# A recurrent layer in fp32: the input parts and the output matmuls on column tiles of 64 in place of 32

## The reference

```python
Xz, Xr, Xh = X @ Wxz.T + bxz, X @ Wxr.T + bxr, X @ Wxh.T + bxh   # for all steps
def step(H, (xz, xr, xh)):
    Z = sigmoid(xz + H @ Whz.T + bhz)
    R = sigmoid(xr + H @ Whr.T + bhr)
    H_tilda = tanh(xh + (R * H) @ Whh.T + bhh)
    H_new = Z * H + (1 - Z) * H_tilda
    Y = H_new @ Whq.T + bhq
out = x + Y                                                       # x is [32, 256, 256]
```

## Time and profile before

| | |
|---|---|
| Median of 3 runs | 524.92 us (524.47 to 526.99) |
| Profiled execution: time, span | 523.88 us, 522.0 us |
| TensorE matmul busy | 510.2 us, 98%, 44184 records |
| Weight load busy | 492.3 us, 94%, 44184 records |
| VectorE, ScalarE busy | 317.6 us (61%), 329.2 us (63%) |
| DMA over the span | 53 GB/s |

### The profile page before, as it was taken

One profiled execution on the slowest core, in us unless ns is written; L12 is line 12 of the kernel. 1 busy time (PEld: TensorE's weight loads), 2 busy tenths in 40 slices (PEclk: granted clock), 3 DMA queues, 4 the chain that ended last, 5 costly groups with the idle time before them and its releaser, 6 DMA issues.

```text
span 522.0 us, 96066 instructions
## 1 busy us (share of the span) xinstructions
PE 510.2 (98%) x44184; PEld 492.3 (94%) x44184; DVE 317.6 (61%) x1929; ACT 329.2 (63%) x1800; POOL 0.2 (0%) x4
## 2 busy tenths in 40 slices
PE   8499999999999999999999999999999999999997
PEld 7499999999999999999999999999999999999997
DVE  1266666666666666666666666666666666666665
ACT  2266666666666666666666666666666666666665
POOL 0000000000000000000000000000000000000000
PEclk9999999999999999999999999999999999999999
DMA  5111121111111111111221111111111111111111
GB/s 176 29 51 45 50 55 46 50 55 45 51 55 45 51 54 45 52 54 45 53 53 45 55 51 45 54 51 45 55 50 45 55 51 45 55 50 45 55 50 51
DMA packets 57735, 27.63 MB, mean 53 GB/s; under 512 B 6784, under 2 KB 56832, under 8 KB 57728
## 3 DMA queue, kind: packets, MB, share of 16 engines
q1 hardware_dynamic: 56880, 26.70, 18.4%
q10 hardware_dynamic: 848, 0.83, 0.5%
HBM read 18.98 MB, written 8.52 MB: 53 GB/s over the span
## 4 chain that ended last, share of the span: by engine, by line
PE 96%; issue 2%; DMA 1%; SPq 0%; DVE 0%; ACT 0%; ACTq 0%; DVEq 0%
PE r_ps L244 34%; PE c_ps L244 28%; PE z_ps L244 23%; PE y_ps L244 11%; DMA whq_sb<-in_whq_dram 1%; SPq L114 0%; SPq L115 0%; SPq L116 0%; SPq L112 0%; DVE u_sb L230 0%; DVE o_sb L212 0%; DVE h_sb L235 0%; ACT c_sb L189 0%; DVE rh_sb L225 0%; ACT r_sb L179 0%
## 5 line engine op out<-in xcount | busy, mean ns | idle before, releaser
L244 PE MATMUL c_ps<-xt_sb,wx_sb 128*32 128x64 f32 (+1 forms) x4104 | 172.8, 225 | 1.5 <-issue 1.5
L244 PE MATMUL z_ps<-xt_sb,wx_sb 128*32 128x64 f32 (+1 forms) x4104 | 163.3, 220 | 0.0
L179 ACT ACTIVATE r_sb<-r_ps 128x32 f32<-128x32 f32 x512 | 91.3, 198 | 106.1 <-PE r_ps L244 98.7
L225 DVE TENSOR_TENSOR rh_sb<-r_sb,h_sb 128x32 f32<-128x32 f32 x512 | 89.8, 192 | 85.3 <-ACT r_sb L179 81.1
L244 PE MATMUL z_ps<-h_sb,whz_sb 128*32 128x32 f32 x8192 | 123.9, 198 | 2.2 <-issue 2.2
L244 PE MATMUL c_ps<-rh_sb,whh_sb 128*32 128x32 f32 x8192 | 122.6, 198 | 2.2 <-issue 1.9
L244 PE MATMUL y_ps<-whq_sb,h_sb 128*32 128x128 f32 x2064 | 113.5, 279 | 0.3 <-DVE h_sb L235 0.3
L244 PEld LDWEIGHTS z_ps<-h_sb,whz_sb 128*32 128x32 f32 x8192 | 108.7, 110 | 2.4 <-issue 2.4
L244 PE MATMUL r_ps<-xt_sb,wx_sb 128*32 128x64 f32 (+1 forms) x4104 | 108.2, 219 | 0.0
L230 DVE SCALAR_TENSOR_TENSOR u_sb<-z_sb,c_sb 128x32 f32<-128x32 f32 x512 | 75.2, 188 | 53.5 <-ACT c_sb L189 53.5
L244 PEld LDWEIGHTS z_ps<-xt_sb,wx_sb 128*32 128x32 f32 (+1 forms) x4104 | 101.1, 110 | 0.0
(11 more groups left out here) (27 smaller groups left out, 359.3 us busy)
## 6 DMA issues: line engine op xcount, KB each, us to landing
xt_sb<-in_xt_dram SPq DMA_DIRECT2D x130, 64.0 KB, 1.8
xres_sb<-in_xr_dram SPq DMA_DIRECT2D x130, 64.0 KB, 1.8
out_dram<-o_sb SPq DMA_DIRECT2D x130, 64.0 KB, 1.6
wx_sb<-in_wx_dram SPq DMA_DIRECT2D x3, 256.0 KB, 3.4
whr_sb<-in_whr_dram ACTq DMA_DIRECT2D x1, 256.0 KB, 5.0
whz_sb<-in_whz_dram ACTq DMA_DIRECT2D x1, 256.0 KB, 5.1
whh_sb<-in_whh_dram ACTq DMA_DIRECT2D x1, 256.0 KB, 5.6
whq_sb<-in_whq_dram SPq DMA_DIRECT2D x1, 256.0 KB, 6.4
```

The lines of the kernel that those rows point to most:

```text
L179: nc.scalar.activation(r_sb[:, o], r_ps[:, o, here], ACT.Sigmoid).then_inc(s_r[o], 1)
L225: nc.vector.tensor_tensor(rh_sb[:, k], r_sb[:, k], old[:, k], ALU.mult).then_inc(s_rh[k], 1)
L244: return nc.tensor.matmul(ps, weights, moving, start=start, stop=False, skip_group_check=True, **kw)
```

## The change

`columns` gets a width. The h-side groups keep 32; `x_piece` passes 64, so that an x group is two matmuls with weights of 128 x 64 in place of four of 128 x 32. `y_piece` issues two matmuls with both steps of the chunk as 64 weight columns. The moving operands, the sums, the places in PSUM, the waits and the order of the groups stay as they are. The x parts before the loop keep the full width.

```diff
-            def columns(ps, cols, w, k, o, moving, start=False):
-
-                for j in range(NQ):
-                    last = mm(ps[B * j:B * j + B, cols], w[:, k, P * o + B * j:P * o + B * j + B], moving,
-                              start=start, tile_position=(0, B * j))
+            def columns(ps, cols, w, k, o, moving, width=B):
+
+                for j in range(0, P, width):
+                    last = mm(ps[j:j + width, cols], w[:, k, P * o + j:P * o + j + width], moving, tile_position=(0, j))
                 return last
...
-                return columns(ps, cols, wx_sb[:, gate], k, o, xt_sb[:, p, k])
+                return columns(ps, cols, wx_sb[:, gate], k, o, xt_sb[:, p, k], width=W)
 
             def y_piece(p, k):
 
-                for j in range(NQ):
-                    half, step = divmod(j, CS)
-                    last = mm(y_ps[p][B * j:B * j + B, 0, 0:P], h_sb[:, k, CS * p + step], whq_sb[:, k, P * half:P * half + P],
-                              tile_position=(0, B * j))
+                for half in range(K):
+                    last = mm(y_ps[p][W * half:W * half + W, 0, 0:P], h_sb[:, k, CS * p:CS * p + CS],
+                              whq_sb[:, k, P * half:P * half + P], tile_position=(0, W * half))
                 return last
```

## The result

The change makes the kernel 48% slower: 779.24 us median (778.8 to 779.9, 4 runs) against 525.42 us (524.47 to 526.99, 4 runs), a ratio of 1.4827 with a 95% interval of 1.4802 to 1.4852. The prediction was 814 us, with 540 to 896 as range, and 0.82 for slower.

A forecast was written before the change was run, and what follows sets the result against it. TensorE's own work was taken to set the time in three steps of four, with the other engines close behind. Profiled 523.9 + 307.2 (switches) - 15.6 (u wait) - 1.2 (less code) = 814.3 us, range 540 to 896.

The forecast's parts named there:

- Instructions removed, at 0: Dropping 28 of 172 pairs a step in x and y groups saves nothing, since moving columns set their pace.
- Wider loads, at 0: Loads of 64 weight columns go side by side on two tiles, 0.111 us, hidden beneath the moving columns: cost 0.
- Rival 4: Loads of the two 64-wide tiles run one after another, x groups take 0.222 us: 674 us, chance 0.03.
- The switches, 2048 x 0.15 = 307 us: Eight changes between 32-wide and 64-wide tiles a step, around x and y runs, each cost TensorE 0.15 us.
- an inference: Switches between 32 and 64, and into wider tiles, cost the same as those seen from full width to 32.
- The sign that was named for the holes: In the timeline, idle time put down to issue, eight times a step, at starts about 0.2 us late.
- Rivals 1 and 2 (mixed freely): Tiles of 32 and 64 mix without loss: 524 us, chance 0.12; or seams also close: 515 us, chance 0.06.
- 3 (one direction): Only switches from wide to narrow pay: 661 us; chance 0.13, shared with smaller holes both ways.
- The 0.166 us: Fixed part of the single matmul latency, taken as one drain per switch: 340 us for all, about 847 us total.
- The cover of the u wait, -15.6 us: At step u == 0, switches between c groups and r take 0.6 us, so TensorE's 0.26 us wait for u disappears.
- Less code, -1.2 us: Four issue pauses in the first iterations, 7.5 us together, shrink with the 112 of 688 pairs removed per iteration.

The follow-up runs named there:

- all64: The changed kernel with the h-side groups on tiles of 64 too, so no width change in the loop: 685.3 us, 1.3046 times the kernel before.
- x_full: The kernel before with the loop's x parts over the full width of 128, y and h side on 32: 1445.78 us, ratio 2.7546.
- mixed: The kernel before with each x group as one tile of 64 and two of 32, y on 32: 1090.29 us, ratio 2.0755.
- x_only: The changed kernel with y back on tiles of 32, only the x parts on 64: 728.52 us, 1.3868 times the kernel before.

## Why the prediction was right

**Instructions removed, at 0.** Right. Half the records of x and y went and no group got faster; an x group behind another still takes 0.11 us.

**Wider loads, at 0.** Right inside a run, wrong at its head: the cover was there only when the load could run ahead. The first wide group of each run pays about 0.05 us, 4 x 256 x 0.05 = 51 us that the prediction didn't see as a term; its dearer hole happened to hold them. Rival 4, loads one after another, is out: all64 has 0.11 us a group and not 0.22.

**The switches, 2048 x 0.15 = 307 us.** The mechanism and the count were right. The size was 0.133 us in the mean, 272 us: the hole is 0.10 us after the last column has gone in and not the 0.15 read from full width against 32, which x_full has too where it leaves full width; the exposed load at the head of each run brings part of it back. Kernels with three and four runs a step give 0.248 to 0.264 us for the two ends of a run. Of what was an inference, that both directions pay is shown by the holes between c and Z (into wide tiles), R and zh, and y and r (out of them); that 32 against 64 costs as much as full width against 32 is wrong by a third. The sign that was named for the holes, idle time put down to issue eight times a step, came only once a step; the starts of the groups show the rest. Rivals 1 and 2 (mixed freely) and 3 (one direction) are refuted. The rule of the Trainium skill, TensorEngine Tiling (Array Packing), section Key Properties, that a change of tiling mode drains TensorE, agrees with every run here in which the width changes, with mixed above all: a change between tiles that share no column costs the same. The 0.166 us, an estimate of one drain from the formula of the Trainium skill, TensorE: Matmul & The Clock Gate, section Single matmul latency, was too much: the hole is 0.10 us behind tiles of 64 and of 32.

**The cover of the u wait, -15.6 us.** The saving is there and smaller, and its cause was wrong twice. From y to r it was 0.41 us in that step and 0.22 in others, so 64 x 0.19 = 12 us could be saved; after, it is 0.37 in every step. x_only shows that the pause was not a wait for u. Nor do the holes cover it: x_only has six of them a step and keeps the pause, all64 has none and is rid of it. That the term came out near is luck.

**Less code, -1.2 us.** Under-sized: the four pauses of 7.5 us became three of 0.73, 0.76 and 1.13 us, 4.9 us less.

So the forecast of 814 us lay 35 us too high, and nearly all of it is the size of a change: 2048 x (0.15 - 0.133) = 35 us. With the measured terms: 522.0 + 2048 x 0.133 - 12 - 5 = 777.4, against a span of 777.0. The 0.133 is fitted to it; that it isn't only a fit shows in the pieces of one step, 3.01 - 1.92 = 1.09 us, which over 8 changes is 0.136 us.

## What to carry to other kernels

On an array cut into column tiles, count the places where the width changes between neighbours in the written order, before counting matmuls: here each cost 0.13 us, more than an x group takes. Keep one width throughout, or bring what has the other width together into fewer runs, where the order of the work allows it (here three in place of four were worth 53 us). Fewer instructions buy nothing where the moving columns already set the pace of a group, and that can be read from two groups of different length with the same number of instructions. And a view of waits names the last semaphore, which need not be the cause: look whether the value was there long before.

## What the hardware showed that was not expected

- The clock of TensorE can fall and not come back in a kernel whose matmul records leave no gap: x_full ran at a granted clock of 0.50 from about 11 us to its end, while the profiled execution of the kernel before went through pauses of up to 2.24 us and stayed at 1.00. In x_only it fell too, to 0.50 from 18 to 22 us, and was back at 1.00 from 25 us on. What decides between these is not shown.
- A loop body twice as long (about 1400 pairs of records in place of 688) went with 6.28 MB in place of 0.10 over the instruction queue in its 32 rounds, and 1450 us in place of 525, part of it by a lower clock (0.753).
- A loop of one round on TensorE costs about 0.13 us in the one kernel and nothing in the other. The pause at the end of the loop is 0.18 to 0.19 us with y on tiles of 32 and nothing with y on tiles of 64.
